# Tokens of an expert round: fetched by row number instead of gathered by matrix products

## The reference, cut to what matters

```python
x = x + _L0_xattn_ref(_layernorm(x), ctx_2048, mask)
x = x + _L0_attn_ref(_layernorm(x), w_qkv, w_out, q_gain)
x = x + _L0_ffn_ref(_layernorm(x), gate_w, gate_proj_w, up_proj_w, down_proj_w)

# _L0_ffn_ref, with H=512, I=192, E=64, K=8
router_logits = x @ gate_w
routing_weights, selected = jax.lax.top_k(router_logits, K)
routing_weights = jax.nn.softmax(routing_weights, axis=-1)
# every token's row goes to each of its 8 experts:
gate = ragged_dot(hidden_sorted, gate_proj_w, group_sizes)
up = ragged_dot(hidden_sorted, up_proj_w, group_sizes)
down = ragged_dot(jax.nn.silu(gate) * up, down_proj_w, group_sizes)
out = sum over the 8 of (down * routing weight)
```

## Time and profile before

| | us |
|---|---|
| median of 3 runs (346.24, 347.84, 349.86) | 347.84 |
| the profiled execution's own time | 346.62 |
| its span, first to last instruction | 344.9 |
| TensorE busy in the span | 318.5 (92%) |
| VectorE busy | 169.0 (49%) |
| ScalarE busy | 86.4 (25%) |
| GpSimd busy | 50.9 (15%) |

### The profile page before, as it was taken

The page is one execution under the profiler, slowest core; times in us unless marked ns, Lnnn a source line. Parts: engine busy times, 40 slices in busy tenths (PEclk is TensorE's granted clock), DMA queues, the critical chain, the costliest instruction groups (busy, mean ns, idle before and its releaser), DMA issues.

```text
span 344.9 us, 8908 instructions
## 1 busy us (share of the span) xinstructions
PE 318.5 (92%) x3086; PEld 179.8 (52%) x3086; DVE 169.0 (49%) x505; ACT 86.4 (25%) x169; POOL 50.9 (15%) x113
## 2 busy tenths in 40 slices
PE   0599999898999888999999999999999999999994
PEld 0453544355775345555566555565555565555561
DVE  7752375764696864343444434344334434344433
ACT  1121301205583334122122122222121222121221
POOL 5000002400000233111111211112111112111110
PEclk9999999997699969999999999999999999999999
DMA  2899997800000005909999308995994999999901
GB/s 66 292 402 392 391 361 246 307 1 3 0 2 2 0 0 172 373 6 320 398 391 390 147 0 315 395 383 167 395 391 168 379 390 392 390 392 391 381 17 62
DMA packets 39755, 83.38 MB, mean 242 GB/s; under 512 B 4648, under 2 KB 12976, under 8 KB 39600
## 3 DMA queue, kind: packets, MB, share of 16 engines
q1 hardware_dynamic: 39312, 82.99, 64.7%
q10 hardware_dynamic: 416, 0.04, 0.1%
HBM read 82.49 MB, written 0.52 MB: 241 GB/s over the span
## 4 chain that ended last, share of the span: by engine, by line
PE 81%; DVE 8%; ACT 4%; issue 3%; POOL 1%; DVEq 1%; POOLq 0%; ACTq 0%
PE psum L1218 18%; PE psum L1243 15%; PE psum L1180 12%; PE psum L1155 8%; PE psum L974 4%; PE psum L1013 4%; PE psum L986 4%; PE psum L1074 2%; PE psum L1227 2%; PE psum L1231 2%; PE psum L1104 2%; PE psum L1058 1%; ACT store L870 1%; PE psum L1128 1%; PE psum L450 1%
## 5 line engine op out<-in xcount | busy, mean ns | idle before, releaser
L1218 PE MATMUL psum<-store 128*32 128x384 f32 x896 | 77.4, 486 | 0.7 <-ACT store L912 0.7
L1243 PE MATMUL psum<-store 128*32 128x256 f32 (+1 forms) x672 | 54.0, 454 | 0.0
L1180 PEld LDWEIGHTS psum<-store 128*128 128x128 bf16 x696 | 39.5, 97 | 19.7 <-DVE store L771 11.3
L1218 PEld LDWEIGHTS psum<-store 128*32 128x32 f32 x896 | 28.9, 110 | 37.7 <-issue 32.3
L1180 PE MATMUL psum<-store 128*128 128x128 bf16 x696 | 44.5, 219 | 0.9 <-DVE store L771 0.3
L543 POOL TENSOR_TENSOR store<-store 128x256 f32<-128x256 bf16 x28 | 17.2, 613 | 152.8 <-PE psum L1227 152.2
L933 ACT ACTIVATE y_parts<-psum,w_slot 128x512 fp32r<-128x512 f32 x28 | 19.2, 687 | 74.6 <-PE psum L1243 74.6
L1243 PEld LDWEIGHTS psum<-store 128*32 128x32 f32 x672 | 19.0, 109 | 31.8 <-issue 27.0
L1155 PE MATMUL psum<-y_parts,place_T 128*128 128x512 f32 x116 | 34.3, 416 | 0.9 <-ACT y_parts L933 0.9
L799 DVE TENSOR_SCALAR place_T<-psum 128x256 fp32r<-128x256 f32 x28 | 11.9, 424 | 47.0 <-PE psum L1243 47.0
L912 ACT ACTIVATE store<-psum 128x512 f32<-128x512 f32 x29 | 17.3, 598 | 33.9 <-PE psum L1180 33.9
(11 more groups left out here) (225 smaller groups left out, 339.5 us busy)
## 6 DMA issues: line engine op xcount, KB each, us to landing
store<-n_L_ffn_gate_proj_w_dram SPq DMA_DIRECT2D x64, 384.0 KB, 6.4
store<-in_L_ffn_up_proj_w_dram SPq DMA_DIRECT2D x64, 384.0 KB, 6.6
store<-n_L_ffn_down_proj_w_dram SPq DMA_DIRECT2D x64, 256.0 KB, 6.6
store<-n_L_ffn_down_proj_w_dram SPq DMA_DIRECT2D x64, 128.0 KB, 7.2
store<-in_L_attn_w_qkv_dram SPq DMA_DIRECT2D x1, 3072.0 KB, 15.2
store<-in_ctx_dram SPq DMA_DIRECT2D x2, 1024.0 KB, 6.7
store<-in_L_attn_w_out_dram SPq DMA_DIRECT2D x1, 1024.0 KB, 17.5
x_sb<-in_x_dram SPq DMA_DIRECT2D x1, 512.0 KB, 4.3
```

Source lines behind the costliest of these rows:

```text
L1180: last = pe.matmul(bank[3][:, c * P:(c + 1) * P], xparts[:, h, part, c, :], chosen_slots[:, h], start=(k == 0), stop=(k == 3 * TH - 1))
L1218: last = pe.matmul(bank[0][quarter, 0:2 * INTER], xs[:, c, quarter], w[:, :, c, :], start=(c == 0), stop=(c == DC - 1))
L1243: last = pe.matmul(bank[6][quarter, cols], hidT[:, k, quarter], ring[r][:, e, at:at + cols.stop - cols.start], start=(k == 0), stop=(k == 2))
```

## The change

`xn` is also stored to a DRAM tensor (`x_dram`), by SP. For each round, two small products of the pick table with a column of token numbers give the row number of each of the 128 slots in PSUM. DVE copies them to `row_no`, and POOL issues an indirect DMA, which fetches 128 rows of 512 f32 into `x_rows`. TensorE transposes them in four steps into the same bank as before. The first round is still gathered by products.

The `mix_t` table and its two f32 transposes are gone. Instead the pick table (now in a ring of four) is multiplied by the bf16 identity, which gives its transpose, and by a table of the routing weights of the team's four experts in three bf16 parts (`w_early`, `w_late`), which gives 12 numbers per slot; DVE keeps those of the slot's own expert with `lane` and sums them to `w_slot`. POOL makes the three parts, once for the first three teams and once for the others. The `mix` of the round before moves to directly behind the gate and up products. Team 0 runs at least two rounds (`least`).

Lines that are left out are new names, memory and semaphores.

```diff
--- before.py
+++ after.py
...
+PICKS = 4
...
+        tok_b = sb("tok_b", [P, TH], BF16)
+        row_no = sb("row_no", [P, 1], I32)
+        least = sb("least", [1, TEAMS])
+        x_dram = nc.dram_tensor("x_normed_rows", (TOK, D), F32)
@@ -167,10 +175,13 @@
         rw, rank = rw_rank[:, 0], rw_rank[:, 1]
         turned = carve([P, 2, TH, EXP_N])
         flipped = carve([P, 2, TH, P])
-        pick_t = carve([P, TH, TEAM, BLK], BF16)
-        pick_0 = carve([P, TH, TEAM, BLK], BF16)
+        picks = carve([P, PICKS * TOK], BF16)
         apart = carve([P, TH, TEAM, BLK])
-        mix_t = carve([P, TH, TEAM, BLK])
+        w_rest = carve([P, TH, EXP_N])
+        w_early = carve([P, TH, 3, FIXED], BF16)
+        w_late = carve([P, TH, 3, EXP_N], BF16)
+        w_lanes = carve([P, 3, TEAM])
+        x_rows = carve([P, D])
         xs = carve([P, DC, P])
         silu = carve([P, INTER])
         hid = carve([P, 2 * P])
...
@@ -378,6 +395,9 @@
                 load_team(range(r * TEAM, (r + 1) * TEAM), r)
             sp.wait_ge(s_x1, 2)
             load_team(range((EARLY - 1) * TEAM, EARLY * TEAM), EARLY - 1)
+            for h in range(TH):
+                sp.wait_ge(s_xn, 2 * TH + h + 1)
+                sp.dma_start(x_dram[h * P:(h + 1) * P, :], xn[:, h]).then_inc(s_xd, 16)
             sp.wait_ge(s_op, 2)
             sp.wait_ge(s_cnt, 2)
             load_team(team_of(word_of(EARLY)), EARLY)
...
@@ -519,38 +542,57 @@
                 pool.wait_ge(s_xp2, h + 1)
                 pool.tensor_tensor(xparts[:, h, 2], rest[:, h], xparts[:, h, 1], ALU.subtract).then_inc(s_xp, 1)
 
+            def weight_parts(src, dst, columns):
+                part = w_rest[:, :, 0:columns]
+                zeros = zero[:, :].unsqueeze(2).to_broadcast([P, TH, columns])
+                ch.step(pool.tensor_tensor(dst[:, :, 0], src, zeros, ALU.subtract))
+                ch.step(pool.tensor_tensor(part, src, dst[:, :, 0], ALU.subtract))
+                ch.step(pool.tensor_tensor(dst[:, :, 1], part, zeros, ALU.subtract))
+                pool.tensor_tensor(dst[:, :, 2], part, dst[:, :, 1], ALU.subtract).then_inc(s_wp, 1)
+
             pool.wait_ge(s_tables, 11)
+            pool.wait_ge(s_rw, 1)
+            weight_parts(rw[:, :, 0:FIXED], w_early, FIXED)
+            pool.wait_ge(s_xd, 32)
             pool.wait_ge(s_rk, 1)
-            pool.wait_ge(s_rw, 1)
             pool.wait_ge(s_cnt, 1)
             step = pool.alloc_register("pool_step")
-            pool.reg_mov(step, 0)
-
-            def rounds_of(q, table):
+            pool.reg_mov(step, 1)
+
+            def differences(ranks, slots):
+                return pool.tensor_tensor(apart, ranks.unsqueeze(3).to_broadcast([P, TH, TEAM, BLK]),
+                                          slots.unsqueeze(1).to_broadcast([P, TH, TEAM, BLK]), ALU.subtract).then_inc(s_ap, 1)
+
+            def fetch_rows(u):
+                pool.wait_ge(s_idx, u)
+                pool.wait_ge(s_xg, u)
+                pool.tensor_tensor(ready[:, :], zero[:, :], zero[:, :], ALU.subtract).then_inc(s_rdy, 1)
+                pool.indirect_dma_start(x_rows, None, x_dram[:, :], bass.IndirectOffsetOnAxis(ap=row_no[:, :], axis=0)).then_inc(s_gat, 16)
+
+            def rounds_of(q, ranks, first=0):
                 count = pool.value_load(rounds[0:1, bass.ds(q, 1)], min_val=1, max_val=TOK // BLK)
-                cols = bass.ds(q * TEAM, TEAM)
-
-                def over_slots(t):
-                    return t[:, :, cols].unsqueeze(3).to_broadcast([P, TH, TEAM, BLK])
-
-                with pool.Fori(0, count) as r:
-                    v = pool.snap(step)
-                    slots = slot_no[:, bass.ds(r, 1), :].unsqueeze(1).to_broadcast([P, TH, TEAM, BLK])
-                    pool.wait_ge(s_pk, v + 1)
-                    pool.tensor_tensor(apart, over_slots(table[:, 1]), slots, ALU.subtract).then_inc(s_ap, 1)
-                    pool.wait_ge(s_pk, v + 2)
-                    pool.wait_ge(s_mtp, v + 1)
-                    pool.tensor_tensor(mix_t, pick_t, over_slots(table[:, 0]), ALU.mult).then_inc(s_mx, 1)
+                with pool.Fori(first, count) as r:
+                    u = pool.snap(step)
+                    pool.wait_ge(s_pk, u)
+                    differences(ranks[:, :, bass.ds(q * TEAM, TEAM)], slot_no[:, bass.ds(r, 1), :])
+                    fetch_rows(u)
                     pool.reg_add(step, step, 1)
 
-            with pool.Fori(0, EARLY) as q:
-                rounds_of(q, rw_rank)
+            rounds_of(0, rank, first=1)
+            with pool.Fori(1, EARLY) as q:
+                rounds_of(q, rank)
             pool.wait_ge(s_tn, 1)
+            weight_parts(turned[:, 0], w_late, EXP_N)
             with pool.Fori(EARLY, TEAMS) as q:
-                rounds_of(q, turned)
-
-            pool.wait_ge(s_pk, pool.snap(step) + 1)
-            pool.tensor_tensor(apart, apart, apart, ALU.subtract).then_inc(s_ap, 1)
+                rounds_of(q, turned[:, 1])
+
+            final = turned[:, 1, :, EXP_N - TEAM:], slot_no[:, 0:1, :]
+            u = pool.snap(step)
+            pool.wait_ge(s_pk, u)
+            differences(*final)
+            fetch_rows(u)
+            pool.wait_ge(s_pk, u + 1)
+            differences(*final)
 
         @block.vector
         def _(dve):
@@ -589,6 +631,9 @@
             dve.tensor_copy(half_of_xnT(1), chunks(7)).then_inc(s_xnd, 1)
...
+            ch.step(dve.tensor_reduce(lane[:, :], ident[:, :].rearrange("p (e s) -> p e s", e=TEAM), AX.X, ALU.add), wait=False)
+            for h in range(TH):
+                ch.step(dve.tensor_scalar(tok_b[:, h:h + 1], col_i[:, :], float(h * P), None, ALU.add), wait=False)
 
             dve.wait_ge(s_plan, 1)
             n = dve.value_load(plan[0:1, 15:16], min_val=1, max_val=NG // 2)
...
@@ -751,14 +794,18 @@
             dve.scalar_tensor_tensor(rank, bank[2][:, 0:TH * EXP_N].rearrange("p (h e) -> p h e", h=TH), 1.0,
                                      chosen_b, ALU.add, ALU.mult).then_inc(s_rk, 1)
             dve.wait_ge(s_rk, 1)
-            dve.tensor_tensor(pick_0, rank[:, :, 0:TEAM].unsqueeze(3).to_broadcast([P, TH, TEAM, BLK]),
-                              slot_no[:, 0:1, :].unsqueeze(1).to_broadcast([P, TH, TEAM, BLK]), ALU.is_equal).then_inc(s_pk0, 1)
+            def pick_of(slot):
+                return picks[:, slot * TOK:(slot + 1) * TOK].rearrange("p (h e s) -> p h e s", h=TH, e=TEAM)
+
+            for u, done in ((0, s_pk), (1, s_pk1)):
+                dve.tensor_tensor(pick_of(u), rank[:, :, 0:TEAM].unsqueeze(3).to_broadcast([P, TH, TEAM, BLK]),
+                                  slot_no[:, u:u + 1, :].unsqueeze(1).to_broadcast([P, TH, TEAM, BLK]), ALU.is_equal).then_inc(done, 1)
 
             dve.wait_ge(s_lst, 1)
-            dve.wait_ge(s_set, TEAMS // 2 + TEAM)
+            dve.wait_ge(s_set, TEAMS // 2 + TEAM + 2)
             lists = bank[1][0:1, 0:2 * EXP_N]
             ch.step(dve.tensor_reduce(cnt_i[:, :], lists[:, EXP_N:].rearrange("p (q e) -> p q e", e=TEAM), AX.X, ALU.max))
-            ch.step(dve.tensor_scalar(cnt_i[:, :], cnt_i[:, :], -1.0, 0.0, ALU.add, ALU.max))
+            ch.step(dve.scalar_tensor_tensor(cnt_i[:, :], cnt_i[:, :], -1.0, least[:, :], ALU.add, ALU.max))
             ch.step(dve.tensor_scalar(cnt_i[:, :], cnt_i[:, :], BLK.bit_length() - 1, None, ALU.arith_shift_right))
             ch.step(dve.tensor_tensor(spare[:, 0:TEAMS], cnt_i[:, :], radix[:, :], ALU.mult))
             with nc.allow_low_precision(reason="whole numbers below 2**24"):
@@ -767,12 +814,18 @@
                 dve.wait_ge(s_pks, 1)
                 ch.step(dve.tensor_tensor(spare[:, :], lists[:, 0:EXP_N], lane_radix[:, :], ALU.mult))
                 dve.tensor_reduce(team_word[:, :], spare[:, :].rearrange("p (q e) -> p q e", e=TEAM), AX.X, ALU.add).then_inc(s_cnt, 1)
-            def write_pick():
-                dve.tensor_scalar(pick_t, apart, 0.0, None, ALU.is_equal).then_inc(s_pk, 1)
-
+            def write_pick(slot):
+                dve.tensor_scalar(picks[:, bass.ds(slot * TOK, TOK)], apart.rearrange("p h e s -> p (h e s)"), 0.0, None,
+                                  ALU.is_equal).then_inc(s_pk, 1)
+
+            def write_rows():
+                dve.tensor_copy(row_no[:, :], bank[7][:, 0:1]).then_inc(s_idx, 1)
+
+            dve.wait_ge(s_idp, 1)
+            write_rows()
             dve.wait_ge(s_cnt, 1)
             dve.wait_ge(s_ap, 1)
-            write_pick()
+            write_pick(1)
             step = dve.alloc_register("dve_step")
             dve.reg_mov(step, 0)
             with dve.Fori(0, TEAMS) as q:
@@ -780,9 +833,7 @@
                 with dve.Fori(0, count):
                     v = dve.snap(step)
                     dve.wait_ge(s_ap, v + 2)
-                    dve.wait_ge(s_xg, v + 1)
-                    dve.wait_ge(s_mx, v + 1)
-                    write_pick()
+                    write_pick((v + 2) & (PICKS - 1))
```

(58 more changed lines are left out.)

24 lines of the change are left out of this document (17 added, 7 removed).

## The result

The kernel after takes **362.38 us** (median of 4 runs, 361.51 to 363.69) against 347.05 us for the kernel before (4 runs, 346.24 to 349.86): ratio **1.043, 95% interval 1.036 to 1.050**. It is slower by 15 us; the forecast was 338 us, 9 us faster, and the result lies 0.4 us above the top of the range. The rival that came true is the first, "the fetch sets the round".

A forecast was written before the change was run, and what follows sets the result against it. TensorE's queue bounds the kernel at 7.29 us a round; at 6.41, weight loads take over, ending the last round at 327.5, plus 2 for the clock: 329.5 against 338.9, 9.4 less, 337.2, rounded to 338 us; range 331 to 362.

The forecast's parts named there:

- the fetch sets the round: Rival: fetch latency above 4.8 us makes each round 1.6 us plus that latency; 367 us at 6.4; chance 22% above 5.8.
- The fetch, which is the disputed step: One row fetch in flight closes a loop from row transposes to landing: 1.6 us plus latency, hidden up to 4.8.
- G: Time from POOL's issue of the row fetch to its landing: 4.1 us, up to 4.8 in full stretches, 4.4 middle.
- The term for sharing the DMA engines: Part of the fetch latency: 0.7 us, the transfer time of 0.262 MB at 391 GB/s counted again.
- The upper bound: For the fetch's landing time: 384 KB loads behind a full queue landed in 7.4 us.
- the lower one: For the fetch's landing time: the store of x_sb, the same 256 KB, landed in 2.2 us on an idle DMA.
- The loop's overhead: Fetch loop without the fetch latency: row transposes, wait for hidT's tails, DVE's copy, POOL's wake and small step; 1.6 us.
- TensorE's round: Products and transposes on TensorE per loop round: 6.41 us instead of 7.29, alone 24.6 us less over 28 rounds.
- The weights take the bound: Late rounds: shorter rounds wait for weight loads, last landed at 321.1, last round ends 327.5; 13 us of TensorE's gain lost.
- The clock: Waits for weights may lower TensorE's clock in the last round: between 0 and 3.4 us, 2 taken.
- The one-time costs: Stores of xn nothing, early weight split nothing, late split 0.4 us once, team 0's minimum of two rounds nothing.
- the late split of the weights: Four POOL steps of 128 columns, 1.9 us behind a fetch, delaying hid 0.4 us once, later taken up by weight waits.

The follow-up runs named there:

- light loads: The changed kernel, with the weight loads of teams 4 to 15 bringing only the first 32 columns of each piece: 329.18 us, against 350.09 for the kernel before.
- a shallow queue of loads: The changed kernel, with SP letting each expert's four weight loads land before it issues the next expert's (teams 4 to 15): 437.49 us.
- fillers: The changed kernel with four unused bf16 products of 512 columns (0.85 us) on TensorE right ahead of its wait for fetched rows: 367.28 us, ratio 1.054.

## Why the prediction was wrong, point by point

**The step that failed** is the one named "The fetch, which is the disputed step": G was taken as 4.1 to 4.8, 4.4 in the middle; it measured 3.4 at least, 6.3 in the median, 7.3 at most. Its terms can be told apart. An idle store of 2.2 plus 1.2 for GpSimd's list gives 3.4, and the fetch beside light loads takes 3.3 to 3.6: right (the instruction itself is 0.97 us). The term for sharing the DMA engines was 0.7 us, the transfer time once more. It is 2.9 us in the median and up to 3.9, and it is no longer transfer: 2.6 us of it pass before the first packet of the rows moves (4.3 us after the issue for 1.7). Why the rows wait there is not shown. That one term turned a gain of 9 us into a loss of 15. Its argument was that the 7.4 us of a load behind a full queue are mostly SP's own queue, and the fetch goes through another. The other queue helped little: 6.3 is nearer to 7.4 than to 2.2, and half the bytes bring it down by 0.6 only. The upper bound was the row that shared the condition which mattered, loads in full flow; the lower one shared the size.

**The loop's overhead**, forecast at 1.6 us, measured 1.60, but by other steps, so the agreement is luck. The forecast had DVE's copy wait for the tails of hidT. In the rounds that wait for their fetch these tails are done before the rows land (at 302.91, for a landing at 303.04), and the copy waits for the row transposes, 0.75 us instead of 0.45, and for the row numbers behind them.

**The rival's price.** By the rival's rule, 1.6 + 6.3 = 7.9 a round, and 28 x (7.9 - 7.29) = 17 us, 364 us for a measured 362.4. The mechanism is the rival's; that the sum is so near is in part luck. The mean of 27 rounds, 7.89, is that of six free rounds of 6.5 to 6.7 and 21 of 8.26 on average, and the loss comes as 4.1 us in the first round and 12.0 in the others. The chance of 22% on that mechanism was the mistake, not its working.

**TensorE's round**: forecast 6.41, measured 6.50 to 6.51 where nothing waits. New transposes 0.48 (forecast 0.45), place, weights and row numbers 0.13 + 0.03 + 0.03 = 0.19 (forecast 0.37), transposes of hid 0.27 (0.22), mix 1.12 (0.93). The bf16 products cost half of their forecast, and mix took it back. Its products are no longer than before (421 ns busy each, for 416), but in their new place they overlap less with what stands ahead: before, they started 0.24 us ahead of the end of hid's transposes (203.51, 203.75), now 0.07 ahead of the end of gate and up (207.61, 207.68). The gather stood in that place before, and took 1.47 us there for 1.36 behind hid's transposes. Why a product overlaps less there was not tested.

**The weights take the bound**: it did not come. At 7.9 us a round they are never waited for, and from 290 to 326 us DMA moves 392 GB/s with the fetches, for 391 before, so the rows do travel within the same 390. With the fetch's delay gone (light loads) the loads were gone too, so no run shows the forecast's 327.5.

**The clock**: forecast 2 us in the last round, behind waits for weights. It came instead in six rounds spread over the loop, behind waits for rows (mean clock 0.79 to 0.81). Most of what it took the fetch had taken already; the estimate above leaves 3 us to it, 1.8 of them in one of the last rounds.

**The one-time costs** were rightly nothing but two. The first fetch was issued at 132.69 (forecast 133.25), yet landed only after 6.8 us, for 4.4, and TensorE waited 3.45 us for it and went on at a lower clock (its down took 3.37 us for 1.86): the first down ended at 143.74, for a forecast of 140.1. And the late split of the weights cost 0.9 us where 0.4 was forecast: from the end of the third down (156.95) to that of the fourth (165.43) it is 8.48 us, 1.97 more than a free round, of which the tables take 1.05 on TensorE.

**The rules that the prediction drew on.** The trace has 3.4 us for the shortest fetch and 6.3 for the median. By the Trainium skill, DMA: Bandwidth & Descriptors, Anatomy of one DMA, the estimate was 2.6 us; the trace disagrees, by 0.8 us where DMA has holes and by 3.7 beside the loads. The fetch instruction takes about the same each time, 0.96 to 1.13 us over 28, and the same steps of DVE stand beside it when loads are light and it lands in 3.6. So what the Trainium skill, SBUF — State Buffer, Who interferes with whom, says of DVE shutting GpSimd out of writing descriptors is not what stretched G here.

## What to carry to other kernels

Before work of a busy engine is handed to a small transfer, look at what the DMA engines do at the moment it must fly, not at what the same transfer takes on idle ones: price it by the row that shares the load, even if its size is another. Then write down the loop it closes. With one fetch in flight its latency and all steps from landing to the next issue are one round, and every engine's saving inside that round is worth nothing until the loop is shorter than it. If only one fetch fits, its chance to lose should be set by how far its latency may rise before the loop is longer than the round, here to 4.8 from an idle 3.4, against the 7.4 of a row under full load.

## What the runs showed of the hardware

- A fetch of 128 rows of 2 KB by row number landed 3.6 us (median, 3.3 at least) after its issue beside light traffic and 6.3 us (median) beside weight loads at 390 GB/s. Half the bytes gave 5.7, half the rows 6.0, a shallow queue of loads 4.7. The difference lies ahead of the first packet: it started 1.7 us after the issue beside light traffic and 4.3 beside full loads, whatever the size of the fetch. GpSimd's instruction took 0.97 us for 128 rows and 0.91 for 64.
- With full fetches among the loads the total rate stayed at 392 GB/s (290 to 326 us; 391 before), and with half the bytes per row at 390: they cost the stream no more than their bytes, while the stream made them land nearly twice as late. With 64 rows in place of 128 the total was 374; no run tells why.
- In six rounds the granted clock fell for part of the round, each time after a wait of 1.4 to 3.45 us for a fetch; but waits of 1.95, 1.76 and 1.51 us (ended at 224.20, 240.56 and 311.41) were not followed by one. With fillers ahead of the wait only the first round was lower (0.82), and the kernel got no faster.
